# Four message-passing layers on one core: an attention pass with paired short operations, and sage passes of 42 slot groups with one chunk of gathered edges each

## The chip, the cores and the metric

The kernel runs on one core of a Trainium2 chip. The metric is the time of one execution on the device in microseconds (us). Engines are named as in the profile: PE is TensorE's matmuls, PEld its weight loads, DVE VectorE, ACT ScalarE, POOL GpSimd, SP SyncE.

## The reference

12500 nodes with 64 features and 200000 edges, sorted by target. Four layers, each a layernorm, a relu, a graph operation and a residual sum. The change touches the second and third:

```python
# layer 1 (attention), for every edge (row, col), Wh = h @ W + b
sim = dot(Wh[row], Wh[col]) / max(|Wh[row]| * |Wh[col]|, 1e-8)
weight = adj * softplus(...) * (row != col) * (c0 * relu(sim) - c1 * relu(-sim))
prop = segment_sum(weight[:, None] * Wh[col], row)
# layer 2 (sage, applied twice)
mean = segment_sum(h[src], dst) / max(deg, 1)
h = relu(mean @ W_l + b_l + h @ W_r)
```

Layer 0 is an edge network (message pass), layer 3 a softmax attention over incoming edges.

## The kernel before

**Two ways to sum over edges.** The message pass and the softmax pass go by *chunks*: 196 chunks of 1024 edges (8 of 128) in the order of the targets. GpSimd gathers the source rows from memory (indirect DMA, 128 rows at a time, 8 for a chunk), a one-hot matrix tells TensorE which of 128 targets from `base_i[c]` on an edge belongs to, and the product is added to `acc`.

The attention pass and the two sage passes go by *slots*, without gathers. The edges are cut into 53 groups of 3840 (`NGR`; the last one adds only 320 edges). Within a group each edge has a slot in one of 49 source blocks of 256 nodes (`NSB`), 128 slots a block. `build_slots` writes, once, a row of slot sources (`srow`, `pair_rows`) and a column of slot targets (`dcol`).

**Sage pass** (`slot_sums`, called twice). The node table `T` lies in SBUF as three bf16 pieces whose sum is the value. `run_steps` writes the program of each engine: in step k each stage with lag l handles item k - l. A group has 25 steps of two source blocks. DVE makes the source one-hots `ohT` for 10 blocks at once (L1685, two operations) and the target one-hots `ohd` for each block (L1691, 256 wide, two per step). PE multiplies `ohT` with `T` (L1728), ACT copies the product from PSUM to `G` (L1717), PE multiplies `ohd` with `G` and sums over the whole group (L1740). Then DVE adds the three pieces (L1701), PE turns the result (L1752) and DVE adds it to a window of 256 columns of `acc` (L1711). Rings of 5 steps tie the engines together: DVE's `ohd` of step k waits for PE's sum of step k - 5.

**Attention pass** (`att_slots`). 49 blocks of source nodes, 8 steps a block; a step takes 7 groups (the last 4) of one block, 392 steps in all. In each, DVE makes four one-hot comparisons (L1524), PE gathers both ends of the edges (L1573) and turns one-hots (L1583, L1590), ACT copies, DVE multiplies (L1532), takes a maximum (L1534) and a sum over 64 features (L1535). From these the weight is made by five short operations on 128 x 7 numbers: reciprocal L1537, product L1540, the two halves L1542 and L1543, their sum L1547. Each waits for the one before. L1503 multiplies rows by the weight, ACT and DVE split the result into three pieces (L1491, L1509, L1496, L1514), and PE sums (L1602).

**Around them.** `phase` runs the node phases (layernorm, weights), 10 groups of nodes each; a phase may also store rows to memory (L349), and waits at its end until they have landed (L623). After the second sage pass a block loads the edge columns of the softmax pass again: targets from the kept copy, sources from the input (L2060 to L2062). Blocks end with all engines meeting.

The round counts (`rounds2_i`) are 1 for the inputs at hand; a pass is repeated only where a block has more than 128 edges of a group or a window is too narrow.

## Time and profile before

| | us |
|---|---|
| median of 3 runs | 9413.38 (9408.04 to 9417.32) |
| the profiled execution | 9405.75 |
| its span, first to last instruction | 9403.0 |
| attention pass, 2805.8 to 4933.1 | 2127.3 |
| first sage pass, 5088.9 to 5976.7 | 887.8 |
| second sage pass, 6142.1 to 7028.1 | 886.0 |
| busy over the span: PE / DVE / ACT / POOL | 7528.1 / 6605.3 / 3741.7 / 3350.5 |

Busy in tenths, in 40 slices of 235 us:

```profile
PE   6577577777768888888886999899995778878777
DVE  3999344444338999999996999689983555555554
ACT  1000222222225656665654777467761222222221
POOL 2677777777500000000000000000001777777774
```

A digit is the busy share of a slice. The attention pass is slices 12 to 20, the sage passes are 21 to 25 and 26 to 29; POOL is idle in all of them. Left of them lies the message pass, right the softmax pass.

### The profile page before, as it was taken

The page shows a single profiled execution, that of the slowest core. Times are in us where ns is not written, and L with a number is a line of the kernel's source. Part 1 is how long each engine was busy: PE and PEld are TensorE (multiplying, and loading weights), DVE is VectorE, ACT ScalarE, POOL GpSimd, SP SyncE. Part 2 cuts the span into 40 slices and gives each one's busy share as a digit, 9 for nine tenths or more (in the row PEclk, how much of TensorE's full clock was granted, in tenths as well). Part 3 has the DMA queues.
Part 4 walks back from the last instruction along what each step waited for, and adds up shares of the span by engine and source line. Part 5 has one row for each costly group of instructions (what it writes and reads, how often), then busy time and mean ns, then how long its engine had stood idle before and what let it go on. Part 6 is the DMA issues. An engine that isn't in the chain of part 4 may idle for free. (4 is left out here: it accounts for less than half of the span.)

```text
span 9403.0 us, 265151 instructions
## 1 busy us (share of the span) xinstructions
PE 7528.1 (80%) x91323; PEld 7064.7 (75%) x91323; DVE 6605.3 (70%) x19944; ACT 3741.7 (40%) x6989; POOL 3350.5 (36%) x3255
## 2 busy tenths in 40 slices
PE   6577577777768888888886999899995778878777
PEld 6344577777657888888876999799984777777776
DVE  3999344444338999999996999689983555555554
ACT  1000222222225656665654777467761222222221
POOL 2677777777500000000000000000001777777774
PEclk9767788888759999999996999799995777777776
DMA  5311222222113222222221333123322111111111
GB/s 64 52 39 40 67 72 73 72 72 73 49 39 101 83 85 84 85 84 84 84 71 48 98 98 98 40 92 99 98 86 24 27 26 26 26 26 26 26 26 29
DMA packets 635318, 586.40 MB, mean 62 GB/s; under 512 B 377638, under 2 KB 481158, under 8 KB 634696
## 3 DMA queue, kind: packets, MB, share of 16 engines
q1 hardware_dynamic: 528824, 461.21, 17.9%
q0 software_dynamic: 104272, 117.41, 6.2%
q8 instruction: 424, 6.95, 0.3%
q10 hardware_dynamic: 1728, 0.25, 0.0%
q14 instruction: 70, 0.57, 0.0%
HBM read 538.95 MB, written 39.60 MB: 62 GB/s over the span
## 5 line engine op out<-in xcount | busy, mean ns | idle before, releaser
L787 POOL DMA_INDIRECT soft_G<-soft,soft_idx x1568 | 1555.6, 992 | 539.1 <-issue 473.0
L657 POOL MEMSET acc<- 96x1280 f32 x30 | 34.4, 1162 | 4638.2 <-POOLq L1330 2447.9
L1717 ACT ACTIVATE sage_G<-ps 128x384 bf16<-128x384 f32 (+1 forms) x2650 | 1284.2, 485 | 508.2 <-PE ps L1728 500.3
L1728 PE MATMUL ps<-T,sage_ohT 128*128 128x192 bf16 x10388 | 1305.5, 247 | 21.4 <-DVE sage_ohT L1685 17.8
L1740 PE MATMUL ps<-sage_G,sage_ohd 128*128 128x192 bf16 x10388 | 1287.1, 245 | 1.0 <-ACT sage_G L1717 1.0
L787 POOL DMA_INDIRECT msg_G<-msg_src,msg_idx x1176 | 1153.1, 981 | 364.2 <-issue 348.7
L1691 DVE TENSOR_SCALAR sage_ohd<-iota,sage_cols 128x256 bf16<-128x256 bf16 x5194 | 1140.8, 282 | 96.1 <-PE ps L1740 66.8
L1573 PE MATMUL ps<-att_far,att_ohT 128*128 128x65 bf16 x15582 | 945.1, 196 | 319.7 <-DVE att_ohT L1524 269.3
L1573 PEld LDWEIGHTS ps<-att_far,att_ohT 128*128 128x128 bf16 x15582 | 689.5, 100 | 389.3 <-DVE att_ohT L1524 283.1
L1573 PE MATMUL ps<-acc,att_ohT 128*128 128x65 bf16 x15582 | 942.0, 196 | 0.5 <-issue 0.5
L1728 PEld LDWEIGHTS ps<-T,sage_ohT 128*128 128x128 bf16 x10388 | 904.8, 98 | 34.6 <-DVE sage_ohT L1685 18.1
L1740 PEld LDWEIGHTS ps<-sage_G,sage_ohd 128*128 128x128 bf16 x10388 | 899.3, 97 | 1.7 <-ACT sage_G L1717 1.4
L896 PE MATMUL ps<-msg_OH,msg_msg 128*65 128x128 f32 x3136 | 475.4, 316 | 376.9 <-ACT msg_msg L941 376.9
L896 PEld LDWEIGHTS ps<-msg_OH,msg_msg 128*65 128x65 f32 x3136 | 420.8, 162 | 392.8 <-ACT msg_msg L941 392.8
L1573 PEld LDWEIGHTS ps<-acc,att_ohT 128*128 128x128 bf16 x15582 | 689.3, 99 | 1.2 <-issue 0.7
L927 DVE TENSOR_TENSOR msg_msg<-ps,msg_G 128x512 f32<-128x512 f32 x196 | 135.4, 691 | 770.5 <-DMA msg_G<-msg_src,msg_idx 761.0
L998 POOL DMA_INDIRECT acc<-msg_src,srci x392 | 526.3, 1343 | 370.5 <-POOLq L306 161.2
L1820 PE MATMUL ps<-ident,soft_G 128*128 128x128 f32 x1568 | 324.6, 375 | 373.2 <-DMA soft_G<-soft,soft_idx 373.2
L941 ACT ACTIVATE msg_msg<-msg_msg 128x512 f32<-128x512 f32 x196 | 123.5, 630 | 1078.2 <-DVE msg_msg L927 1078.2
L1685 DVE TENSOR_SCALAR sage_ohT<-sage_rows,iota_p 128x1280 bf16<-128x1280 bf16 (+1 forms) x1060 | 529.2, 542 | 32.4 <-PE ps L1728 20.4
L1820 PEld LDWEIGHTS ps<-ident,soft_G 128*128 128x128 f32 x1568 | 256.5, 192 | 390.1 <-DMA soft_G<-soft,soft_idx 390.1
L1602 PE MATMUL ps<-att_Vp,att_ohs 128*128 128x192 bf16 x5194 | 493.9, 246 | 9.9 <-issue 5.2
(443 smaller groups left out, 15924.3 us busy)
## 6 DMA issues: line engine op xcount, KB each, us to landing
sage_rows<-srow SPq DMA_DIRECT2D x424, 320.0 KB, 3.3
acc<-pair_rows SPq DMA_DIRECT2D x196, 448.0 KB, 3.7
att_rows<-pair_rows SPq DMA_DIRECT2D x147, 448.0 KB, 3.7
msg_edge<-edge_attr SPq DMA_DIRECT2D x196, 256.0 KB
sage_rows<-srow SPq DMA_DIRECT2D x106, 288.0 KB, 3.3
soft_G<-soft,soft_idx POOLq DMA_INDIRECT x1568
msg_G<-msg_src,msg_idx POOLq DMA_INDIRECT x1176
kept_rows<-acc POOLq DMA_DIRECT2D x49, 256.0 KB, 2.4
```

The lines of the kernel that those rows point to most:

```text
L787: eng.indirect_dma_start(B["G"][h][:, j, :], None, src_table, bass.IndirectOffsetOnAxis(ap=B["idx"][h][:, j:j + 1], axis=0)).then_inc(gath ...
L896: ins = pe.matmul(ps[0:m, 6 + h % 2, 0:P], rows(j), B["OH"][h % HOTS][:, j, :], start=(j == 0), stop=(j == TPC - 1))
L927: dve.tensor_tensor(B["msg"][b][:, :, 0:D], ps[:, 4 + b, :].rearrange("p (j d) -> p j d", d=D), B["G"][h][:], ALU.add).then_inc(S["summed" ...
L998: pool.indirect_dma_start(kept_G[q % KRING][:, j, :], None, msg_src, bass.IndirectOffsetOnAxis(ap=srci[:, kept_chunks[q], j:j + 1], axis=0 ...
L1573: ins = pe.matmul(ps[:, bank + s % 2, c * W65:(c + 1) * W65], ohT[s % 2][:, f, half, c * P:(c + 1) * P], rows_of[:, half, k, :], start=(ha ...
L1602: ins = pe.matmul(ps[:, 4 + s // QS, half * 3 * D:(half + 1) * 3 * D], ohs[s % 4][:, c, half * P:(half + 1) * P], Vp[s % 4][:, c, :], star ...
L1685: ins = dve.tensor_scalar(ohT[b][:, half, 0:w], rows[ring][:, 0:w], iota_p1[:, half:half + 1], None, ALU.is_equal)
L1691: ins = dve.tensor_scalar(ohd[s % RING][:, c, :], iota256[:], cols[s // STEPS][:, 2 * q + c:2 * q + c + 1], None, ALU.is_equal)
L1717: act.activation(G[s % RING][:, 0:m, :], ps[:, s % RING, 0:m * 3 * D].rearrange("p (c n) -> p c n", c=m), ACT.Copy).then_inc(S["taken"], 1)
L1728: ins = pe.matmul(ps[:, s % RING, c * 3 * D:(c + 1) * 3 * D], ohT[b][:, half, at:at + P], T[:, 2 * (2 * q + c) + half, 0:3 * D], start=(ha ...
L1740: ins = pe.matmul(ps[:, 5 + s // STEPS, half * 3 * D:(half + 1) * 3 * D], ohd[s % RING][:, c, half * P:(half + 1) * P], G[s % RING][:, c, ...
L1820: pe.transpose(banks(2)[:, j, :], B["G"][h][:, j, D + 1:D + 2].broadcast_to([P, P]), ident[:])
```

## The change

**Attention.** `t` and `weight` are twice as wide. `dve_weight` is cut in two: `dve_dot` (product, maximum, sum) runs each step and writes its half of `t`; the five short operations run in odd steps only, over both halves. The product by the weight, `dve_v`, moves from lag 1 to lag 2, and ACT's first copy of it, `act_hi`, from the head of its step to the end.

On DVE, attention pass before, from the last operations of one step (`keep` holds the weighted rows, `att_t` the short columns):

```order
L1532 TENSOR_TENSOR acc<-ps,att_C 128x455
L1534 TENSOR_SCALAR att_t<-acc 128x7
L1535 TENSOR_REDUCE att_t<-acc 128x7
L1537 RECIPROCAL att_t<-att_t 128x7
L1540 TENSOR_TENSOR att_t<-att_t 128x7
L1542 SCALAR_TENSOR_TENSOR att_t<-att_t,att_own 128x7
L1543 SCALAR_TENSOR_TENSOR att_t<-att_t,att_own 128x7
L1547 TENSOR_TENSOR att_weight<-att_t 128x7
L1503 TENSOR_TENSOR keep<-att_C,att_weight 128x448
```

The same engine and place now, from the end of one step (up to L1519) over the next one into its chain:

```order
L1555 TENSOR_SCALAR att_t<-acc 128x7
L1556 TENSOR_REDUCE att_t<-acc 128x7
L1519 TENSOR_TENSOR keep<-att_C,att_weight 128x448
L1540 TENSOR_SCALAR att_ohT<-acc,iota_p 128x896 x4
L1525 TENSOR_TENSOR keep<-keep,att_Vp 128x448
L1530 TENSOR_TENSOR att_Vp<-keep,att_Vp 128x7x64
L1552 TENSOR_TENSOR acc<-ps,att_C 128x455
L1555 TENSOR_SCALAR att_t<-acc 128x7
L1556 TENSOR_REDUCE att_t<-acc 128x7
L1565 RECIPROCAL att_t<-att_t 128x14
L1568 TENSOR_TENSOR att_t<-att_t 128x14
L1570 SCALAR_TENSOR_TENSOR att_t<-att_t,att_own 128x14
```

L1519 follows L1556 at once where a step has no chain; the five operations stand in every second step, over 14 columns.

**Sage.** `XG` = 42: only the first 42 groups (161280 edges) go by slots. The last 42 chunks hold the other edges; the first 3 of them and half of the fourth overlap the slot groups, and their targets are set to a number that matches nothing. Each slot group carries one chunk, 42 in a pass. GpSimd issues 8 gathers of 128 rows x 384 bytes for it from a new table `sage_rows` in memory, into one of two buffers. DVE makes a one-hot of the chunk (two operations), PE multiplies 24 times (8 parts, three pieces) into bank 7, and DVE adds the result to `acc`. No group stands behind the loop any more: 21 iterations of two groups.

On DVE in the sage loop now, where a chunk's one-hot is made and a group is added:

```order
L1762 TENSOR_SCALAR sage_chunk_off<-chunk_dst,base_bc 128x8
L1766 TENSOR_TENSOR sage_chunk_oh<-chunk_iota,sage_chunk_off 128x1024
L1109 REGISTER_ALU
L1727 TENSOR_SCALAR sage_ohd<-iota,sage_cols 128x256 x2
L1721 TENSOR_SCALAR sage_ohT<-sage_rows,iota_p 128x1152 x2
L1109 REGISTER_ALU
L1727 TENSOR_SCALAR sage_ohd<-iota,sage_cols 128x256 x2
```

The first two rows are new, once a group; a third new one, `acc<-acc,ps 64x128` (L1777), stands 15 steps behind them. On PE, the products of a chunk stand three at a time behind the two sums of a step:

```order
L1821 MATMUL ps<-sage_G,sage_ohd 128x192 x4
L1789 MATMUL ps<-sage_chunk_oh,sage_chunk_rows 64x128 x3
L1809 MATMUL ps<-T,sage_ohT 128x192 x4
L1821 MATMUL ps<-sage_G,sage_ohd 128x192 x4
L1789 MATMUL ps<-sage_chunk_oh,sage_chunk_rows 64x128 x3
```

This is so in 8 of a group's 25 steps; the first of them waits for the gathers and the one-hot.

**Around.** The two node phases ahead of the sage passes store `T` into `sage_rows`. A block ahead of them loads the chunk columns and builds a comparison table. The source indices are kept in memory in SBUF's layout (`src_kept`) and loaded from there later on. A block ahead of each sage pass sets the chunk bases; GpSimd's semaphores are brought back after it. `slot_rounds` works out a second pair of round counts.

The diff, cut to its core:

```diff
+XG = 42
...
-            sp.dma_start(node_rows(table, g), group_of(T, g) if buf == "T" else src_of[buf][s][:, :, 0:cols]).then_inc(out_sem[k][s], 16)
+            sp.dma_start(node_rows(table, g), group_of(T, g)[:, :, 0:cols] if buf == "T" else src_of[buf][s][:, :, 0:cols]).then_inc(out_sem[k][s], 16)
...
+            dve.tensor_tensor(gstate[:, 12:13], gstate[:, 1:2], small[:, 7:8], ALU.max)
...
-        t, weight, red = buf("t", [P, 6, PC], F32, 1)[0], buf("weight", [P, PC], F32, 4), buf("red", [P, 2, D], F32, 1)[0]
+        t, weight, red = buf("t", [P, 6, 2 * PC], F32, 1)[0], buf("weight", [P, 2 * PC], F32, 2), buf("red", [P, 2, D], F32, 1)[0]
...
-            dve.wait_ge(S["weight"], n + 1)
+            dve.wait_ge(S["weight"], pair_of(i, s) + 1)
             need(dve, S["lo"], n - 3)
-            w = weight[s % 4][:, 0:m].rearrange("p (c o) -> p c o", o=1).broadcast_to([P, m, D])
+            w = weight[s // 2 % 2][:, s % 2 * PC:s % 2 * PC + m].rearrange("p (c o) -> p c o", o=1).broadcast_to([P, m, D])
             dve.tensor_tensor(V[s % 4][:, 0:m, :], C_[s % 4][:, 0:m, 0:D], w, ALU.mult).then_inc(S["v"], 1)
...
+        def dve_dot(dve, i, s):
+            b, q, n, m = place(i, s)
+            at = slice(s % 2 * PC, s % 2 * PC + m)
+            dve.wait_ge(S["taken"], n + 1)
+            need(dve, S["guard"], n)
+            need(dve, S["dot"], n)
+            dve.tensor_tensor(prod[:, 0:m, :], ps[:, s % 2, 0:m * W65].rearrange("p (c d) -> p c d", d=W65), C_[s % 4][:, 0:m, :], ALU.mult).then_inc(S["prod"], 1)
+            dve.wait_ge(S["prod"], n + 1)
+            need(dve, S["weight"], pair_of(i, s))
+            dve.tensor_scalar(t[:, 0, at].rearrange("p (c o) -> p c o", o=1), prod[:, 0:m, D:W65], 1.0e-8, None, ALU.max).then_inc(S["guard"], 1)
+            dve.tensor_reduce(t[:, 1, at], prod[:, 0:m, 0:D], AX, ALU.add).then_inc(S["dot"], 1)
+
         def dve_weight(dve, i, s):
             b, q, n, m = place(i, s)
-            k = s // QS
-            mine = own[k][:, :, q * PC:q * PC + m]
-            dve.wait_ge(S["taken"], n + 1)
-            dve.tensor_tensor(prod[:, 0:m, :], ps[:, s % 2, 0:m * W65].rearrange("p (c d) -> p c d", d=W65), C_[s % 4][:, 0:m, :], ALU.mult).then_inc(S["prod"], 1)
-            dve.wait_ge(S["prod"], n + 1)
-            dve.tensor_scalar(t[:, 0, 0:m].rearrange("p (c o) -> p c o", o=1), prod[:, 0:m, D:W65], 1.0e-8, None, ALU.max).then_inc(S["guard"], 1)
-            dve.tensor_reduce(t[:, 1, 0:m], prod[:, 0:m, 0:D], AX, ALU.add).then_inc(S["dot"], 1)
+            if s % 2 == 0:
+                return
+            p, w = pair_of(i, s), PC + m
+            mine = own[s // QS][:, :, (q - 1) * PC:(q - 1) * PC + w]
             dve.wait_ge(S["guard"], n + 1)
-            dve.reciprocal(t[:, 2, 0:m], t[:, 0, 0:m]).then_inc(S["recip"], 1)
+            dve.reciprocal(t[:, 2, 0:w], t[:, 0, 0:w]).then_inc(S["recip"], 1)
             dve.wait_ge(S["dot"], n + 1)
-            dve.wait_ge(S["recip"], n + 1)
-            dve.tensor_tensor(t[:, 3, 0:m], t[:, 1, 0:m], t[:, 2, 0:m], ALU.mult).then_inc(S["sim"], 1)
-            dve.wait_ge(S["sim"], n + 1)
-            dve.scalar_tensor_tensor(t[:, 4, 0:m], t[:, 3, 0:m], 0.0, mine[:, 0, :], ALU.max, ALU.mult).then_inc(S["pos"], 1)
-            dve.scalar_tensor_tensor(t[:, 5, 0:m], t[:, 3, 0:m], 0.0, mine[:, 1, :], ALU.min, ALU.mult).then_inc(S["neg"], 1)
-            dve.wait_ge(S["pos"], n + 1)
-            dve.wait_ge(S["neg"], n + 1)
+            dve.wait_ge(S["recip"], p + 1)
+            dve.tensor_tensor(t[:, 3, 0:w], t[:, 1, 0:w], t[:, 2, 0:w], ALU.mult).then_inc(S["sim"], 1)
+            dve.wait_ge(S["sim"], p + 1)
+            dve.scalar_tensor_tensor(t[:, 4, 0:w], t[:, 3, 0:w], 0.0, mine[:, 0, :], ALU.max, ALU.mult).then_inc(S["pos"], 1)
+            dve.scalar_tensor_tensor(t[:, 5, 0:w], t[:, 3, 0:w], 0.0, mine[:, 1, :], ALU.min, ALU.mult).then_inc(S["neg"], 1)
+            dve.wait_ge(S["pos"], p + 1)
+            dve.wait_ge(S["neg"], p + 1)
             need(dve, S["v"], n - 3)
-            dve.tensor_tensor(weight[s % 4][:, 0:m], t[:, 4, 0:m], t[:, 5, 0:m], ALU.add).then_inc(S["weight"], 1)
+            dve.tensor_tensor(weight[s // 2 % 2][:, 0:w], t[:, 4, 0:w], t[:, 5, 0:w], ALU.add).then_inc(S["weight"], 1)
...
-                flow(dve, (0, dve_turned), (3, dve_rest), (4, dve_lo), (6, dve_add), (1, dve_weight), (1, dve_v))
+                flow(dve, (0, dve_turned), (3, dve_rest), (4, dve_lo), (6, dve_add), (1, dve_dot), (1, dve_weight), (2, dve_v))
...
-                flow(act, (2, act_hi), (1, act_one_hots), (3, act_mid), (0, act_take), (0, act_next))
+                flow(act, (1, act_one_hots), (3, act_mid), (0, act_take), (0, act_next), (2, act_hi))
...
-    run_steps(eng, 2 * STEPS, NGR // 2, STEPS, stages)
+    run_steps(eng, 2 * STEPS, XG // 2, 0, stages)
...
+            dve.wait_ge(S["cadd"], g + 1)
             w = acc[0:D, bass.ds(first, SB)]
             dve.tensor_tensor(w, w, ps[0:D, 7, 0:SB], ALU.add).then_inc(S["added"], 1)
+
+        def pool_chunks(pool):
+            for n in range(XG):
+                need(pool, S["csum"], n - 1)
+                for j in range(TPC):
+                    pool.indirect_dma_start(chunk_rows[n % 2][:, j, :], None, sage_rows, bass.IndirectOffsetOnAxis(
+                        ap=chunk_src[:, n, j:j + 1], axis=0)).then_inc(chunk_in[n % 2], 16)
+
+        def dve_chunk(dve, i, s):
+            n, k = i * 2 + s // STEPS, s // STEPS
+            if s % STEPS:
+                return
+            need(dve, S["coh"], n - 1)
+            dve.tensor_scalar(chunk_off[k][:], chunk_dst[:, bass.ds(n, 1), :].rearrange("p o j -> p (o j)"), base_bc[:, bass.ds(n + (C - XG), 1)], None, ALU.subtract).then_inc(S["coff"], 1)
+            need(dve, S["csum"], n - 1)
+            dve.wait_ge(S["coff"], n + 1)
+            pairs = chunk_off[k][:].rearrange("p (a o t) -> p a o t", o=1, t=2).broadcast_to([P, TPC // 2, P, 2])
+            dve.tensor_tensor(chunk_oh[k][:], chunk_iota[:], pairs, ALU.is_equal).then_inc(S["coh"], 1)
+
+        def dve_chunk_add(dve, i, s):
+            n = i * 2 + s // STEPS
+            if s % STEPS:
+                return
+            first = dve.value_load(base_i[0:1, bass.ds(n + (C - XG), 1)], min_val=0, max_val=N)
+            dve.wait_ge(S["csum"], n + 1)
+            need(dve, S["added"], n)
+            need(dve, S["cadd"], n)
+            w = acc[0:D, bass.ds(first, P)]
+            dve.tensor_tensor(w, w, ps[0:D, 7, SB:SB + P], ALU.add).then_inc(S["cadd"], 1)
+
+        def pe_chunk(pe, i, s):
+            n, k, j = i * 2 + s // STEPS, s // STEPS, s % STEPS
+            if j >= TPC:
+                return
+            if j == 0:
+                need(pe, S["added"], n)
+                need(pe, S["cadd"], n)
+                pe.wait_ge(S["coh"], n + 1)
+                pe.wait_ge(chunk_in[k], (i + 1) * (16 * TPC))
+            for part in range(3):
+                ins = pe.matmul(ps[0:D, 7, SB:SB + P], chunk_rows[k][:, j, part * D:(part + 1) * D], chunk_oh[k][:, j // 2, :, j % 2],
+                                start=(j == 0 and part == 0), stop=(j == TPC - 1 and part == 2))
+            if j == TPC - 1:
+                ins.then_inc(S["csum"], 1)
...
-                flow(dve, (0, dve_one_hots), (11, dve_reduce), (21, dve_add))
+                flow(dve, (0, dve_one_hots), (18, dve_chunk), (11, dve_reduce), (21, dve_add), (33, dve_chunk_add))
...
-                flow(pe, (0, pe_gather), (2, pe_sum), (16, pe_turn))
+                flow(pe, (0, pe_gather), (2, pe_sum), (16, pe_turn), (23, pe_chunk))
...
+              [(sage_rows, "T", 3 * D, "pieces", 2)])
...
-sp.dma_start(srci[:, 0:C - 1, :], by_edge(a["src"], 0, C - 1)).then_inc(again, 16)
-sp.dma_start(srci[:, C - 1:C, :], by_edge(a["src"], E - CE, 1)).then_inc(again, 16)
-sp.wait_ge(again, 48)
+sp.dma_start(srci[:].rearrange("p c j -> p (c j)"), src_kept[:]).then_inc(again, 16)
```

## Rows read from the trace of the kernel before

**Rows 1.** Busy by stretch: us, PE, PEld, DVE, ACT, POOL, clock, DMA share, GB/s.

```profile
2805.80:4933.10 2127.30, 1819.09 (x41552) 1744.30 (x41552) 1957.61 (x5978) 1258.46 (x2056) 0.00 (x0) 0.97 0.27 85
5088.90:5976.70 887.80, 881.51 (x10494) 874.30 (x10494) 825.66 (x3233) 642.12 (x1325) 0.00 (x0) 1.00 0.32 97
5200.00:5900.00 700.00, 697.23 (x8326) 692.09 (x8324) 654.29 (x2565) 509.41 (x1051) 0.00 (x0) 1.00 0.33 98
6142.10:7028.10 886.00, 882.29 (x10494) 875.07 (x10494) 825.67 (x3233) 642.12 (x1325) 0.00 (x0) 1.00 0.32 97
```

**Rows 2.** Waits from 5200 to 5900 us: total, times, longest.

```profile
DVE sage_ohd L1691 <- PE ps L1740: 24.4, 84, 0.4
DVE sage_ohT L1685 <- PE ps L1728: 10.1, 21, 0.5
```

**Rows 3.** Groups by shape, same stretch: busy us, mean ns, idle before, releaser.

```profile
L1691 DVE TENSOR_SCALAR sage_ohd<-iota,sage_cols 128x256 bf16<-128x256 bf16 x2059 | 452.0, 282 | 35.6 <-PE ps L1740 24.4
L1685 DVE TENSOR_SCALAR sage_ohT<-sage_rows,iota_p 128x1280 bf16<-128x1280 bf16 x338 | 171.1, 550 | 10.1 <-PE ps L1728 10.1
L1701 DVE TENSOR_REDUCE sage_red<-ps 128x128 f32<-128x384 f32 x42 | 23.2, 552 | 0.0
```

**Rows 4.** Timeline of the attention pass at 3504 us: start, length, instruction.

```profile
3503.94 0.19 DVE L1537 RECIPROCAL att_t<-att_t 128x7 f32<-128x7 f32 x1
3504.41 0.46 PEld L1583 LDWEIGHTS ps<-ident_b,att_ohT 128*128 128x128 bf16 x8
3504.83 0.38 PEld L1590 LDWEIGHTS ps<-ident_b,att_ohT 128*128 128x128 bf16 x6
3504.97 0.63 DVE L1503 TENSOR_TENSOR keep<-att_C,att_weight 128x448 f32<-128x448 f32 x1
```

**Rows 5.** Wait of TensorE in the attention pass, 2900 to 4800 us.

```profile
PE ps L1573 <- DVE att_ohT L1524: 252.2, 267, 2.3
```

**Rows 6.** The reciprocal of the attention pass at two widths.

```profile
L1537 DVE RECIPROCAL att_t<-att_t 128x7 f32<-128x7 f32 x311 | 60.1, 193 | 0.0
L1537 DVE RECIPROCAL att_t<-att_t 128x4 f32<-128x4 f32 x45 | 7.6, 168 | 0.0
```

**Rows 7.** GpSimd's gathers: of 300 to 900 us, and of 7300 to 9300 us.

```profile
L998 POOL DMA_INDIRECT acc<-msg_src,srci x297 | 418.4, 1409 | 162.9 <-DMA kept_rows<-acc 83.8 <-issue 79.1
...
L787 POOL DMA_INDIRECT soft_G<-soft,soft_idx x1542 | 1530.6, 993 | 469.9 <-issue 465.7 <-DVE soft_msg L1888 2.7 <-ACT soft_idx L874 1.5
```

**Rows 8.** One line each, all its instructions: min/median/max ns.

```profile
L1860 DVE TENSOR_SCALAR soft_q<-soft_q,soft_win x196: 218/220/461, 7286.6 to 9308.6; 128x2 f32<-128x2 f32 x196
...
L413 DVE TENSOR_SCALAR enter_st<-enter_st x10: 172/172/16002, 25.7 to 178.1; 128x10 f32<-128x10 f32 x10
```

**Rows 9.** Operations like those added: two by line, one from the costliest groups.

```profile
L1208 DVE TENSOR_TENSOR slots_fields<-slots_oh,acc x159: 903/905/921, 286.6 to 936.5; 128x1470 bf16<-128x1470 bf16 x159
...
L1224 DVE TENSOR_TENSOR slots_ohslot<-count_slot,slots_slot x53: 2157/2158/2193, 293.1 to 941.4; 128x3840 bf16<-128x3840 bf16 x53
...
L905 DVE TENSOR_TENSOR acc<-acc,ps 65x128 f32 x196 | 55.6, 284 | 52.2 <-issue 42.4 <-PE ps L896 8.9
```

**Rows 10.** Timeline at two ends of node phases, the first with a store.

```profile
2788.52 0.84 DVE L443 TENSOR_TENSOR T<-after_msg_rN,T 128x650 bf16<-128x650 f32 x1 [0.82 <-ACT T L507]
2799.11 0.36 SPq L1609 DMA_DIRECT2D keep<-bcol  x1
...
5082.48 0.82 DVE L443 TENSOR_TENSOR T<-after_att_xc,T 128x640 bf16<-128x640 f32 x1
5085.04 0.35 SPq L1671 DMA_DIRECT2D sage_cols<-dcol  x1
```

**Rows 11.** Timeline after the second sage pass, and one transfer's issue to landing.

```profile
7064.63 0.33 SPq L2060 DMA_DIRECT2D dstf_again<-dst_kept  x1
7084.10 1.27 ACT L489 ACTIVATE after_sage_accS<-acc 65x1280 f32<-65x1280 f32 x1 [25.35 <-PEq L2057]
...
dstf_again<-dst_kept SPq DMA_DIRECT2D x1, 784.0 KB, 4.5
```

More of the change, by code:

```diff
@@ L81, in gnn_kernel @@
         dst_kept = dram("dst_kept", (P, C * TPC))
+        src_kept = dram("src_kept", (P, C * TPC), I32)
+        sage_rows = dram("sage_rows", (NPAD, 3 * D), BF16)
         rec_b = dram("rec_b", (NGR, P, KF * TG), BF16)
@@ L112, in gnn_kernel @@
         rounds2_i = sb("rounds2_i", [1, 1], I32)
+        rounds3_i = sb("rounds3_i", [1, 1], I32)
+        rebuild3_i = sb("rebuild3_i", [1, 1], I32)
         rebuild_i = sb("rebuild_i", [1, 1], I32)
@@ L1354, in slot_rounds, with next_slots @@
             dve.drain()
-        def next_slots(dve):
+            dve.tensor_tensor(gstate[:, 12:13], gstate[:, 1:2], small[:, 7:8], ALU.max)
+            dve.drain()
+            dve.tensor_tensor(gstate[:, 13:14], gstate[:, 4:5], gstate[:, 12:13], ALU.mult)
+            dve.drain()
+            dve.tensor_scalar(gstate[:, 14:15], gstate[:, 13:14], 1.5, float(NGR - 1), ALU.is_gt, ALU.mult)
+            dve.drain()
+            dve.tensor_scalar(gstate[:, 14:15], gstate[:, 14:15], 1.0, None, ALU.add)
+            dve.tensor_copy(rounds3_i[:], gstate[0:1, 13:14])
+            dve.drain()
+            dve.tensor_copy(rebuild3_i[:], gstate[0:1, 14:15])
+            dve.drain()
+        def next_slots(dve, windows=1):
             r, wrap, w, last = (gstate[:, k:k + 1] for k in (7, 8, 9, 10))
@@ L1366, in next_slots @@
             dve.drain()
-            dve.tensor_tensor(last, w, gstate[:, 1:2], ALU.is_lt)
+            dve.tensor_tensor(last, w, gstate[:, windows:windows + 1], ALU.is_lt)
             dve.drain()
@@ L1451, in act_block @@
                             need(act, S["gathered"], b * QS - QS)
-                            need(act, S["weight"], b * QS - QS)
+                            need(act, S["weight"], b * (QS // 2) - QS // 2)
                             hold(act)
@@ L1651, in place, with _ @@
                     return g, q, i * (2 * STEPS) + s, min(2, NSB - 2 * q)
+                with nc.Block() as block:
+                    @block.vector
+                    def _(dve):
+                        move_bases(dve, True)
                 with nc.Fori(0, rounds) as r:
@@ L1749, in pe_turn @@
                             need(pe, S["added"], g)
+                            pe.wait_ge(S["cadd"], g + 1)
                             hold(pe)
@@ L1769, in _ @@
                                 flow(act, (0, act_take))
+                            @block.gpsimd
+                            def _(pool):
+                                pool_chunks(pool)
                             @block.tensor
                             def _(pe):
-                                flow(pe, (0, pe_gather), (2, pe_sum), (16, pe_turn))
+                                flow(pe, (0, pe_gather), (2, pe_sum), (16, pe_turn), (23, pe_chunk))
                         with nc.Block() as block:
+                            @block.gpsimd
+                            def _(pool):
+                                for q in chunk_in:
+                                    pool.wait_ge(q, XG // 2 * (16 * TPC))
+                                pool.inc_swdge_sem(chunk_in, [XG // 2 * (16 * TPC)] * 2, mode="sub")
                             @block.sync
@@ L2043, in gnn_kernel, with _ @@
         att_slots()
+        chunks_kept = ExitStack()
+        chunk_src = chunks_kept.enter_context(nc.sbuf_tensor("chunk_src", [P, XG, TPC], I32))
+        chunk_dst = chunks_kept.enter_context(nc.sbuf_tensor("chunk_dst", [P, XG, TPC], F32))
+        chunk_iota = chunks_kept.enter_context(nc.sbuf_tensor("chunk_iota", [P, TPC // 2, P, 2], BF16))
+        first_edge = XG * GE - (C - XG) * CE
+        whole, part = first_edge // CE, first_edge % CE // TPC
+        assert XG % 2 == 0 and 0 <= first_edge and whole < XG and part % 32 == 0
+        s_chunks, s_masked = sem("chunk_columns"), sem("chunks_masked")
+        with nc.Block() as block:
+            @block.sync
+            def _(sp):
+                sp.dma_start(chunk_src[:].rearrange("p c j -> p (c j)"), src_kept[:, (C - XG) * TPC:]).then_inc(s_chunks, 16)
+                sp.dma_start(chunk_dst[:].rearrange("p c j -> p (c j)"), dst_kept[:, (C - XG) * TPC:]).then_inc(s_chunks, 16)
+                sp.wait_ge(s_chunks, 32)
+            @block.vector
+            def _(dve):
+                dve.tensor_copy(chunk_iota[:], iota_f[:].rearrange("p (o n t) -> p o n t", o=1, t=1).broadcast_to([P, TPC // 2, P, 2])).then_inc(s_masked, 1)
+                dve.wait_ge(s_chunks, 32)
+                if whole:
+                    dve.memset(chunk_dst[:, 0:whole, :], -4.0 * P).then_inc(s_masked, 1)
+                if part:
+                    dve.memset(chunk_dst[0:part, whole, :], -4.0 * P).then_inc(s_masked, 1)
         phase("after_att", "prop", {"v": [(1, "xc"), (1, "var"), (2, "rest"), (2, "own"), (1, "h"), (2, "lo")],
@@ L2050, in gnn_kernel @@
                                        "p": [(1, "mean"), (2, "own"), (1, "turned")]},
-              [])
+              [(sage_rows, "T", 3 * D, "pieces", 2)])
         slot_sums("sage2")
+        chunks_kept.close()
         tables.close()
```

20 lines of the change are left out of this document (14 added, 6 removed).

## The prediction

> **What bounds the kernel now.** I began with the busy digits in 40 slices and cut the span into stretches. The change works in three of them: the attention pass (2127.3 us) and the two sage passes (887.8 and 886.0 us) [rows 1]. The message pass before them and the softmax pass behind them, both paced by GpSimd's gathers, keep their code.
>
> In the middle of a sage pass TensorE is busy for 697.23 of 700.00 us [rows 1]; 42 groups end in that stretch (one reduction each [rows 3]), so a group lasts 16.67 us and TensorE works 16.60 of them. VectorE is close behind: it waits for TensorE 24.4 + 10.1 us there [rows 2], 0.82 us a group, so its own work is 15.85 us. The reader is to see two engines that lie 5% apart: whatever shortens one hands the pass to the other.
>
> In the attention pass it is the other way round: TensorE is busy 1819.1 of 2127.3 us [rows 1] and waits for VectorE's one-hots [rows 5], while VectorE shows hardly a wait for another engine. Its 392 steps (49 blocks of 8) take 5.4 us each. VectorE sets that time.
>
> **Attention: one chain of short operations for two steps.** From the start of the reciprocal to the start of the product that uses the weight VectorE needs 3504.97 - 3503.94 = 1.03 us [rows 4]: five operations on 7 columns, each waiting for the one before. Two steps now share one chain over 14 columns. Width costs little: the reciprocal goes from 168 to 193 ns for 3 more columns [rows 6], so 7 more are 0.06 us, and I give the other four 0.04 together. A pair saves 2 x 1.03 - 1.13 = 0.93 us, 196 pairs save 182 us. What hides the rest: TensorE's 1819 us fit into the 1945 that remain. The product comes one step later and ScalarE copies it at the end of its step instead of the beginning; VectorE's subtraction, which needs that copy, has the four comparisons of the next step ahead of it. If that cover is thin in some steps, a few us go. Bounds 0 and 182; I take 178.
>
> **Sage: 42 groups instead of 53.** 11 groups go from each pass: at the old pace 11 x 16.67 = 183 us a pass. Each remaining group carries one chunk of 1024 edges.
>
> TensorE gets 24 products of 128 columns. Eight weight loads of such products take 3504.83 - 3504.41 = 0.42 us start to start [rows 4], 0.0525 each, so 1.26 us: 16.60 + 1.26 = 17.86 us a group.
>
> VectorE gets an offset (0.22 us, as L1860 [rows 8]), a comparison over 1024 elements (905 ns at 1470 and 2158 at 3840 elements give 0.53 ns an element, so 0.67 us [rows 9]) and an addition from PSUM (0.28 us, L905 [rows 9]): 1.17 us, hence 15.85 + 1.17 = 17.02 us.
>
> GpSimd gets 8 gathers a group: 993 ns each plus 466/1542 = 0.30 us between two, so 10.4 us; beside the slot building, where VectorE is all but full, 1409 ns and 13.4 us [rows 7]. Both fit into 17.9.
>
> By these sums TensorE would still set the pace. What they leave out is that the two engines disturb each other. A VectorE operation that takes 218 ns at least takes up to 461 when gathers run [rows 8]: a gather holds it up by as much as 0.24 us. In that pass VectorE is mostly doing something else; in the sage pass 93% of its time is busy (654.29 of 700 [rows 1]), nearly all in tensor_scalar operations like that one [rows 3], so that nearly every gather will hit one. The cost for 8 gathers lies between 0 and 1.9 us a group from these rows; I take 0.2 us each, near the top, 1.6 us. VectorE then needs 18.6 us and takes the pace from TensorE by 0.7. A pass: 53 x 16.67 = 883.5 becomes 42 x 18.6 = 781.2, 102.3 less, both 204.6.
>
> The Trainium skill, SBUF — State Buffer, "SBUF: two separate sides", says more than these rows: a VectorE instruction in a 2-port mode and a GpSimd instruction exclude each other for their whole length. The trace agrees for computing instructions (a tensor_scalar of 172 ns took 16002 at the start [rows 8], where GpSimd fills count tables) but not for gathers: 461 ns at most, against gathers of 993. What the whole rule would do is the slower rival below.
>
> **What stands around the passes.** Two node phases now write their table to memory. A phase that does so ends 2799.11 - 2789.36 = 9.75 us behind its last table entry, one that does not 5085.04 - 5083.30 = 1.74 us [rows 10]: +8.0 each, 16. The block that moves the bases ahead of each pass: a change of block is that 1.74, with its operations 3 us, twice 6; 0 and 10 are the bounds. The block that loads the chunk columns: less than half of a 784 KB load, which lands in 4.5 us [rows 11], with its block 6 (3 to 8). Keeping the source indices: another store beside the first, 3 (0 to 4.5). Six more short operations on the round counts: 1.5. Longer tails of both passes, with the semaphore subtraction: 4 (1 to 10). Against it, the sources come back from the kept copy: the old load held everything up for 7084.10 - 7064.63 = 19.5 us; two plain loads should take 7.5, so -12. Together +24.5 us, between 10 and 40.
>
> **Sum.** It is made against the profiled execution, 9405.75 us (span 9403.0): 9405.75 - 178 - 204.6 + 24.5 = 9047.7. The median of the runs is 7.6 us above that execution, so 9055 us as a median.
>
> **Rivals.**
> - TensorE keeps the pace (0.18). Waits for the port fall into the 0.82 us that VectorE has spare, a group takes 17.9: 2 x (883.5 - 751.8) = 263 instead of 205, 8997 us. For it: most gathers in the last pass leave short operations at their median of 220. Against it: VectorE is never that free here.
> - GpSimd starves (0.18). VectorE's operations follow each other without a gap and a gather waits until that row breaks; TensorE then waits for the chunk's rows, and only in that wait does VectorE leave gaps. The mean of 1409 ns beside a full VectorE [rows 7] speaks for some of it. With groups between 18.6 and 22.9, say 20.8 us, both passes gain 2 x (883.5 - 873.6) = 20: 9240 us.
> - The attention gain fails (0.06), because ScalarE's later copy holds up VectorE by as much as was saved: 9055 + 178 = 9233 us. For it: ScalarE is 59% busy with long copies [rows 1]; against it: it has 2 us a step to spare.
> - Slower than before (0.08). A gather keeps VectorE out for its whole 0.99 us. Nearly all of VectorE's operations there are of the kind that can be kept out, so 8 x 0.99 = 7.9 us a group, 17.02 + 7.9 = 24.9 us: 2 x (883.5 - 1045.8) = -325, and 9055 + 205 + 325 = 9585 us. It decides from 22.9 us a group, where the two passes' 1767 us and the other parts' gain of 153.5 are used up ((1767 + 153.5) / 84), that is from 0.73 us lost per gather. This is what the skill's rule of exclusion gives with durations from rows; the 461 ns speak against it. The same page has a gather-side price, 620 ns alone against some 3100 beside a VectorE copy; by that an estimate of 8 x 3.1 = 24.8 us a group on GpSimd would also be slower.
>
> **How the numbers follow.** The forecast has 0.50, and its own range is 9015 to 9110. TensorE's case adds the low side, starvation and the failed attention gain the high side up to some 9235; beyond lie half of starvation and the slower case, and a little below 8975. So 8975 to 9235. About 0.2% (19 us) is what a measurement of this kernel can tell from none. Faster by more: all cases but the last, less a little of starvation's far end, 0.91; same 0.02; slower 0.07.
>
> **What would show it.** In the changed profile: the five short operations with 196 instances each and an attention pass near 1950 us; sage groups counted by their reduction (42 in a pass), 18.6 us apart, with TensorE at some 96% busy instead of 99.6 and waiting for VectorE's one-hots; VectorE's 256-wide comparisons with a mean above 282 ns; gathers between 1.0 and 1.6 us; the chunk's product never waiting for its gathers; 8 us between the last table entry and the pass. The forecast is wrong if TensorE stays at 99% (too high), if TensorE waits for gathers or the comparisons' mean passes some 340 ns (too low), or if VectorE waits for ScalarE in the attention pass.

## The result, and the profile after

The changed kernel takes 9139.98 us (median of 4 runs, 9133.8 to 9148.12), the kernel before 9414.31 (4 runs beside it). The ratio is 0.971, 95% interval 0.9693 to 0.9727. The forecast was 9055, with a range of 8975 to 9235. The profiled execution took 9133.8 us, its span 9132.0.

Busy time by stretch of the changed kernel (us, then PE, PEld, DVE, ACT, POOL, granted clock, DMA share, GB/s), to be held against [rows 1]: the attention pass, the first sage pass, its middle, the second sage pass.

```profile
2817.90:4765.30 1947.40, 1791.03 (x41552) 1726.21 (x41552) 1819.28 (x4999) 1259.69 (x2055) 0.00 (x0) 0.98 0.31 93
4928.80:5765.30 836.50, 832.84 (x9324) 739.94 (x9324) 704.03 (x2689) 508.99 (x1050) 525.46 (x334) 1.00 0.37 101
5200.00:5700.00 500.00, 499.73 (x5606) 443.77 (x5604) 422.98 (x1617) 306.21 (x633) 326.13 (x203) 1.00 0.37 102
5931.10:6767.80 836.70, 833.28 (x9324) 740.16 (x9324) 703.70 (x2689) 508.99 (x1050) 516.57 (x333) 1.00 0.37 101
```

Three things stand there. The attention pass fell by 179.9 us, from 2127.3 to 1947.4. The sage passes fell by only 51.3 and 49.3. And in their middle TensorE is busy for 499.73 of 500 us while VectorE fell to 85%: TensorE sets the pace, more than before. Spans differ by 271.0 us; with 280.5 from the passes, what stands around them costs 9.5.

Waits of the changed kernel in the middle of the sage pass (total us, times, longest), against [rows 2]:

```profile
ACT sage_G L1798 <- PE ps L1809: 192.2, 628, 0.8
POOL sage_chunk_rows L1754 <- PE ps L1789: 119.5, 25, 6.4
DVE sage_ohd L1727 <- PE ps L1821: 58.6, 124, 0.6
PEld ps L1789 <- issue: 31.6, 201, 0.2
PEld ps L1809 <- DVE sage_ohT L1721: 3.6, 15, 0.3
```

All others wait for TensorE, GpSimd too: it waits for the chunk products of two chunks ago, and TensorE never for a gather. One row is new in kind: the weight loads of the chunk products (L1789) stand behind a gap of 0.16 us on average (31.6 us in all), 201 times, that is once for each triple (eight a group). They are not loaded ahead.

Groups by shape in the same stretch (busy us, mean ns, idle before), against [rows 3]:

```profile
L1754 POOL DMA_INDIRECT sage_chunk_rows<-sage_rows,chunk_src x203 | 327.6, 1614 | 174.0 <-PE ps L1789 119.5 <-issue 54.6
L1727 DVE TENSOR_SCALAR sage_ohd<-iota,sage_cols 128x256 bf16<-128x256 bf16 x1236 | 274.9, 284 | 58.9 <-PE ps L1821 58.6
L1789 PE MATMUL ps<-sage_chunk_oh,sage_chunk_rows 128*64 128x128 bf16 x601 | 72.0, 227 | 0.0
L1737 DVE TENSOR_REDUCE sage_red<-ps 128x128 f32<-128x384 f32 x25 | 13.5, 541 | 0.0
```

25 reductions in 500 us give only a rough pace. Finer are the 256-wide comparisons, 49 a group (2059 of them are the 42 groups of [rows 3]): 1236 are 25.2 groups, so a group takes 19.8 us, where I had 18.6 and for TensorE alone 17.86. VectorE's comparison went from 282 to 284 ns. Where TensorE's time goes, two stretches of its own timeline show (start, length, instruction): a step without chunk products, and one with three.

```profile
5301.34 0.49 PE L1821 MATMUL ps<-sage_G,sage_ohd 128*128 128x192 bf16 x4
5301.67 0.33 PE L1809 MATMUL ps<-T,sage_ohT 128*128 128x192 bf16 x2
...
5303.34 0.49 PE L1821 MATMUL ps<-sage_G,sage_ohd 128*128 128x192 bf16 x4
5303.76 0.36 PE L1789 MATMUL ps<-sage_chunk_oh,sage_chunk_rows 128*64 128x128 bf16 x3
5304.05 0.34 PE L1809 MATMUL ps<-T,sage_ohT 128*128 128x192 bf16 x2
```

From the four L1821 to the next L1809 it is 0.33 us, with three products between them 0.71: three products cost 0.38 us, not 3 x 0.0525 = 0.16. Eight times a group that is 3.04 us instead of 1.26. The shape column has the clue: 128*64, the weights are 64 columns wide, among products whose weights are 128 wide.

The short operations of the attention pass, against [rows 6], and the wait that was to be feared there (2900 to 4700 us):

```profile
L1565 DVE RECIPROCAL att_t<-att_t 128x14 f32<-128x14 f32 x139 | 32.0, 230 | 0.0
L1575 DVE TENSOR_TENSOR att_weight<-att_t 128x14 f32<-128x14 f32 x139 | 24.2, 174 | 14.9 <-DVE att_t L1571 4.4
```

```profile
PE ps L1601 <- DVE att_ohT L1540: 98.7, 186, 1.2
DVE keep L1525 <- ACT att_Vp L1507: 15.8, 29, 1.6
```

TensorE's wait for one-hots fell from 252.2 [rows 5] to 98.7 us. VectorE does wait for ScalarE now, 29 times, for 15.8 us in all.

### The profile page after: what moved, and what is told of

The parts are those of the page before. It is cut to its first block and busy times, and to the rows that moved or that the text cites. A ratio compares the mean times of both kernels' runs of the same rounds, so it can differ in the third digit from the quotient of the medians.

```text
span 9132.0 us, 256071 instructions
## 1 busy us (share of the span) xinstructions
PE 7411.1 (81%) x88983; PEld 6783.6 (74%) x88983; DVE 6231.9 (68%) x17891; ACT 3478.7 (38%) x6439; POOL 4407.7 (48%) x3927
## 5 line engine op out<-in xcount | busy, mean ns | idle before, releaser
L1754 POOL DMA_INDIRECT sage_chunk_rows<-sage_rows,chunk_src x672 | 1047.7, 1559 | 732.4 <-PE ps L1789 410.2
L662 POOL MEMSET acc<- 96x1280 f32 x30 | 34.4, 1162 | 2573.7 <-POOLq L2147 2270.4
L1798 ACT ACTIVATE sage_G<-ps 128x384 bf16<-128x384 f32 (+1 forms) x2100 | 1018.0, 485 | 677.4 <-PE ps L1809 671.2
L1809 PE MATMUL ps<-T,sage_ohT 128*128 128x192 bf16 x8232 | 1041.6, 248 | 26.8 <-DVE sage_ohT L1721 25.8
L1727 DVE TENSOR_SCALAR sage_ohd<-iota,sage_cols 128x256 bf16<-128x256 bf16 x4116 | 917.3, 284 | 196.8 <-PE ps L1821 195.2
L1821 PE MATMUL ps<-sage_G,sage_ohd 128*128 128x192 bf16 x8232 | 1020.1, 245 | 0.0
L1809 PEld LDWEIGHTS ps<-T,sage_ohT 128*128 128x128 bf16 x8232 | 668.7, 98 | 107.3 <-DVE sage_ohT L1721 38.5
L1821 PEld LDWEIGHTS ps<-sage_G,sage_ohd 128*128 128x128 bf16 x8232 | 712.2, 97 | 0.6
```

The source lines that it names most:

```text
L1727: ins = dve.tensor_scalar(ohd[s % RING][:, c, :], iota256[:], cols[s // STEPS][:, 2 * q + c:2 * q + c + 1], None, ALU.is_equal)
L1754: pool.indirect_dma_start(chunk_rows[n % 2][:, j, :], None, sage_rows, bass.IndirectOffsetOnAxis(ap=chunk_src[:, n, j:j + 1], axis=0)).the ...
L1798: act.activation(G[s % RING][:, 0:m, :], ps[:, s % RING, 0:m * 3 * D].rearrange("p (c n) -> p c n", c=m), ACT.Copy).then_inc(S["taken"], 1)
L1809: ins = pe.matmul(ps[:, s % RING, c * 3 * D:(c + 1) * 3 * D], ohT[b][:, half, at:at + P], T[:, 2 * (2 * q + c) + half, 0:3 * D], start=(ha ...
L1821: ins = pe.matmul(ps[:, 5 + s // STEPS, half * 3 * D:(half + 1) * 3 * D], ohd[s % RING][:, c, half * P:(half + 1) * P], G[s % RING][:, c, ...
```

## The experiments

Eleven times a kernel was timed, on four chips; each is compared with the kernel before on the same chip. On chip 7 the kernel before takes 9415 us, as it did in the result above: I call this the first kind. On chips 8, 6 and 12 it takes 10289, 10343 and 10286 us: the second kind. That difference became a finding of its own.

| kernel | kind (chip) | us | ratio to before (95%) |
|---|---|---|---|
| attention alone | second (8) | 10103.3 | 0.982 (0.980 to 0.983) |
| wide weights | second (8) | 10280.3 | 0.998 (0.997 to 1.000) |
| adjacent elements | second (8) | 10553.6 | 1.025 (1.023 to 1.027) |
| one step | second (8) | 10632.2 | 1.033 (1.032 to 1.035) |
| changed kernel | first (7) | 9133.3 | 0.970 (0.968 to 0.971) |
| one step | first (7) | 9028.0 | 0.959 (0.958 to 0.961) |
| swapped roles | first (7) | 8938.1 | 0.950 (0.949 to 0.951) |
| two chunks gathered | first (7) | 9132.3 | 0.969 (0.968 to 0.971) |
| swapped, two gathered | second (6) | 9880.5 | 0.955 (0.953 to 0.956) |
| swapped roles | second (6) | 10675.8 | 1.032 (1.030 to 1.034) |
| changed kernel | second (12) | 10560.9 | 1.026 (1.024 to 1.028) |

**Attention alone.** The kernel before with the diff's hunks in `att_slots` only.

> The attention change alone; the sage passes, the stores and all else are as before. The trace gives the attention pass 1947.3 us instead of 2127.3. Theory (the pass gains by itself, and the sage part is what fell short): 9414 - 180 = 9234 us, and the sage passes last 888 and 886 us. Rival (part of the 180 us is due to what else was changed, or is given back after the pass): above 9250 us.

10289.3 to 10103.3: 186 us, where 180 was expected, though the base was another. The attention pass took 1945.6 us (3317.0 to 5262.6) and the sage passes 886.7 and 885.1. So this part gains by itself, and by about the same amount on a slower chip.

**Wide weights.**

```diff
-ins = pe.matmul(ps[0:D, 7, SB:SB + P], chunk_rows[k][:, j, part * D:(part + 1) * D], chunk_oh[k]...
+ins = pe.matmul(ps[:, 7, SB:SB + P], chunk_rows[k][:, j, part // 2 * D:part // 2 * D + 2 * D], chunk_oh[k]...
```

> The changed kernel with weights of 128 columns instead of 64 in the chunk's 24 products (each takes two neighbouring pieces, so the product has 128 rows instead of 64); same number of products, same one-hots, same gathers. Its sums are not the reference's, since pieces are taken twice. Theory A (narrow weights are the cost: they are not loaded ahead, and going from 128 to 64 columns and back costs 172 ns a triple): a product falls from 0.14 to about 0.055 us, TensorE needs 17.9 us a group instead of 20.0, and the time is 9140 - 84 x 2.1 = 8964 us; if VectorE beside the gathers needs 18.6 us, as I had forecast, 9022 us. Theory B (the one-hot is read with a step of two elements, and that makes a product dear): no change, 9140 us.

The time, expected at 8964 or 9022 us on a chip of the first kind, was never taken there. On this chip it settles nothing: the engines are held up in the sage passes (below), and the order of the times does not follow TensorE's work (wide weights 10280, adjacent elements 10554, one step 10632 us). TensorE's timeline in a stretch at full clock (1.00 from 5640 to 5680 us) does settle it:

```profile
5663.52 0.49 PE L1821 MATMUL ps<-sage_G,sage_ohd 128*128 128x192 bf16 x4
5663.85 0.34 PE L1789 MATMUL ps<-sage_chunk_oh,sage_chunk_rows 128*128 128x128 bf16 x3
5664.02 0.33 PE L1809 MATMUL ps<-T,sage_ohT 128*128 128x192 bf16 x2
```

0.50 us instead of 0.71: three wide products cost 0.17 us, 0.057 each. That is my price of 0.0525, nearly. Theory A holds for this stretch; its effect on the time follows from the runs on chip 7.

**Adjacent elements.**

```diff
-chunk_oh[k][:, j // 2, :, j % 2]
+chunk_oh[k][:, j // 2, j % 2 * D:(j % 2 + 1) * D, :].rearrange("p n t -> p (n t)")
```

> The changed kernel, but each chunk product reads 128 neighbouring elements of the one-hot instead of every second one of 256. Its sums are not the reference's, since the elements are in another order. Theory B (the step is the cost): 8964 to 9022 us. Theory A (narrow weights): 9140 us, no change. A mixture, with the step making 18 of the 70.6 ns between two products of a triple: 24 x 0.018 = 0.43 us a group, 9104 us.

```profile
5800.90 0.49 PE L1821 MATMUL ps<-sage_G,sage_ohd 128*128 128x192 bf16 x4
5801.32 0.35 PE L1789 MATMUL ps<-sage_chunk_oh,sage_chunk_rows 128*64 128x128 bf16 x3
5801.61 0.34 PE L1809 MATMUL ps<-T,sage_ohT 128*128 128x192 bf16 x2
```

0.71 us, as with every second element. Reading every second element costs nothing that this shows; theory B falls. The 9140 us expected by theory A could not be seen on this chip (10554).

**One step.** The 24 products of a chunk one behind the other.

```diff
-if j >= TPC: return
+if j: return
 ...
-for part in range(3):
+for j in range(TPC):
+    for part in range(3):
```

> The changed kernel with the 24 chunk products of a group in one step, one behind the other, instead of three in each of eight steps: one change from 128 to 64 columns and back a group instead of eight. Theory A1 (the change between the two widths costs 172 ns each time): 7 x 0.172 = 1.2 us a group less, 9140 - 101 = 9039 us. Theory A2 (a narrow product costs 0.14 us wherever it stands) and theory B (the step): 9140 us.

Its timeline, on chip 8 (10632 us, where 9039 or 9140 stood for a chip of the first kind):

```profile
5927.00 0.49 PE L1821 MATMUL ps<-sage_G,sage_ohd 128*128 128x192 bf16 x4
5927.42 1.55 PE L1790 MATMUL ps<-sage_chunk_oh,sage_chunk_rows 128*64 128x128 bf16 x24
5928.90 0.34 PE L1809 MATMUL ps<-T,sage_ohT 128*128 128x192 bf16 x2
```

24 products cost 1.90 - 0.33 = 1.57 us, three cost 0.38. With a price p for a product and e for going to narrow weights and back, 24p + e = 1.57 and 3p + e = 0.38: p = 0.057, e = 0.21 us. A narrow product costs what a wide one does; the eight changes of width a group cost 8 x 0.21 = 1.7 us. Two equations for two unknowns prove nothing yet. The test is what they say of the time on a chip of the first kind, together with the control:

> The changed kernel once more, beside the other kernels of this call, because the chip of the first four runs took 10289 us for the kernel before instead of 9414. On a chip like the first: ratio 0.971 to the kernel before. On one like the second: the first four runs had ratios of 0.982 (attention alone), 1.025 (adjacent elements, whose triples last as long as those of the changed kernel) and 1.033 (one step), so the changed kernel should be near 1.025 there, slower than before. If the ratio is 0.971 there too, the edits and not the chip explain those two.

> The 24 chunk products in one step again. In its first trace the 24 products follow each other at 57.9 ns, with 176 ns ahead of the first and 151 behind the last, against three at 70.5 ns with the same two edges, eight times, in the changed kernel. TensorE saves 7 x (0.176 + 0.151 - 0.082 - 0.058) = 1.3 us a group by that, so 18.6 us instead of 20.0. On a chip like the first: 9140 - 84 x 1.35 = 9027 us, if no other engine takes over (VectorE at 18.6, as I had forecast, would give the same). On a chip like the second: near 1.033 of the kernel before.

Control: 9133.3, ratio 0.970, as expected. One step: 9028.0 where 9027 was expected; only the order of TensorE's program differs. The sage passes took 785.1 and 786.3 us instead of 836. VectorE at my 18.6 us a group would have given the same time, so it needs one run more to tell these two apart.

**Swapped roles.** The one-hot is the weight, the rows are streamed. VectorE reduces the three pieces (a second small operation beside L1737), TensorE turns the result.

```diff
-for part in range(3):
-    ins = pe.matmul(ps[0:D, 7, SB:SB + P], chunk_rows[k][:, j, part * D:(part + 1) * D], chunk_oh[k][:, j // 2, :, j % 2], ...)
+ins = pe.matmul(ps[:, 7, SB:SB + 3 * D], chunk_oh[k][:, j // 2, :, j % 2], chunk_rows[k][:, j, :], start=(j == 0), stop=(j == TPC - 1))
...
+dve.tensor_reduce(chunk_red[k][:], ps[:, 7, SB:SB + 3 * D].rearrange("p (k d) -> p d k", d=D), AX, ALU.add)
+pe.transpose(ps[0:D, 7, SB:SB + P], chunk_red[k][:], ident[:])
```

> The chunk's one-hot becomes the weights (128 columns) and the gathered rows (192 columns) are what is streamed: 8 products of the usual shape a group instead of 24 narrow ones, then a reduction by VectorE, a turn by TensorE, and the addition as before. TensorE: 16.60 + 8 x 0.084 + 0.3 (turn, with its edges) = 17.6 us; VectorE 16.9 + 0.35 = 17.3. If the edges of narrow weights are the whole excess: 17.7 us a group and 9140 - 84 x 2.3 = 8947 us on a chip like the first. If VectorE beside gathers needs 18.6 + 0.35 us, as my forecast had it: 9052 us. If the chain reduction, turn, addition holds up the group's own turn (all use one bank): 9140 or more.

8938.1 us, where 8947 was expected: 5.0% under the kernel before and the fastest of all. The middle of its first sage pass, 5000 to 5600 us: busy time, and the counts of one operation a group.

```profile
5000.00:5600.00 600.00, 599.15 (x7129) 590.95 (x7126) 578.22 (x2238) 416.47 (x862) 366.98 (x277) 1.00 0.42 116
```

```profile
L1728 DVE TENSOR_SCALAR sage_ohd<-iota,sage_cols 128x256 bf16<-128x256 bf16 x1685 | 373.5, 288 | 3.7
L1738 DVE TENSOR_REDUCE sage_red<-ps 128x128 f32<-128x384 f32 x34 | 18.7, 549 | 0.0
L1775 DVE TENSOR_REDUCE sage_chunk_red<-ps 128x64 f32<-128x192 f32 x34 | 12.2, 358 | 11.8 <-PE ps L1805 11.8
```

1685 comparisons are 34.4 groups in 600 us, 17.4 us each. VectorE does all its work, one reduction more, beside all eight gathers, and is busy for 578.22 / 34.4 = 16.8 us of them. My forecast of 18.6 us for it (19.0 with that reduction) is refuted here, in a pass where it is 96% busy: the whole group is shorter.

**Two chunks gathered.**

```diff
-for n in range(XG):
+for n in range(2):
 ...
-pe.wait_ge(chunk_in[k], (i + 1) * (16 * TPC))
+pe.wait_ge(chunk_in[k], 16 * TPC)
```

> The changed kernel with the gathers of the first two chunks only in each pass; the later products use those rows again, so its sums are not the reference's. If TensorE alone sets the pace and gathers cost the others nothing: no change on a chip like the first, 9140 us. If gathers take time from VectorE that shows in the end: up to 42 x 2 x 0.3 = 25 us less. On a chip like the second, where the gathers seem to hold up everything: the sage passes fall to 836 us each as on the first chip, and the ratio to the kernel before to (10289 - 180 - 100 + 10) / 10289 = 0.974.

9132.3 against 9133.3 us: on chip 7 640 of 672 gathers cost the time nothing that can be measured. The middle of the sage pass without them (5200 to 5700 us), and VectorE's comparison, which takes 284 ns with them:

```profile
5200.00:5700.00 500.00, 499.95 (x5612) 444.16 (x5611) 419.14 (x1614) 305.82 (x632) 0.00 (x0) 1.00 0.26 82
L1727 DVE TENSOR_SCALAR sage_ohd<-iota,sage_cols 128x256 bf16<-128x256 bf16 x1235 | 273.2, 275 | 62.0 <-PE ps L1821 61.8
```

9 ns on 49 comparisons is 0.44 us a group, 0.055 us a gather. That is an upper bound, since VectorE's operations overlap: seven comparisons of 284 ns stand in 1.47 us of the changed kernel's timeline at 5301.58. By busy time the gathers cost it 422.98 - 419.14 = 3.8 us in 25 groups with 203 gathers, 0.02 us each. I had taken 0.2.

**The second kind of chip.** Three runs go with the question why the same kernel loses there.

> The kernel with swapped roles (one-hot as weights), with the gathers of the first two chunks only in each pass; later products use those rows again, so its sums are not the reference's. It was 8938 us with all gathers on a chip like the first, where TensorE was busy 599.15 of 600 us and VectorE 578.22. If gathers take next to nothing from VectorE and TensorE: 8938 us, within 15. If they take 0.2 us each, as I had forecast, VectorE falls to 15.7 us a group and the time stays, since TensorE holds 17.6. On a chip like the second, if gathers in flight hold up the other engines: it keeps the whole gain, ratio near 0.955 to the kernel before, where the version with gathers does not.

> The kernel with swapped roles and all gathers once more, beside the one without. On a chip like the first: ratio 0.950 to the kernel before, again. On one like the second: a group needs about as long as in the other kernels with gathers there; with 1.025 and 1.033 for kernels whose TensorE work is 20.0 and 18.6 us a group, the pace there is not TensorE's work, and I expect 1.00 to 1.03.

> The changed kernel itself, to have its ratio on a chip of the second kind. If the kernel before takes some 10300 us: gathers hold up the other engines there, the kernel with adjacent elements (same pace by TensorE) had 1.025 and the one with swapped roles 1.032 with gathers and 0.955 without, so the changed kernel should have 1.025, that is slower than before. If gathers were not the cause, and it was something in those edits, it should have 0.97. On a chip of the first kind (9414 us for the kernel before): 0.970 once more.

The changed kernel is slower than before there, 1.026 (chip 12). On chip 6 the swapped one gains 4.5% without most of its gathers (sage passes 748.5 us each) and loses 3.2% with them (1148 and 1146 us). Besides the gathers these two differ only in that TensorE no longer waits for later gathers, and no such wait of TensorE shows in the trace with them. VectorE without them is busy for 384.59 us in 400, or 23.1 groups: 16.6 us a group beside 16.8 with them on chip 7, where 0.2 us a gather would have given 15.7. Waits of the changed kernel on chip 12, 5700 to 6100 us of its first sage pass:

```profile
ACT sage_G L1798 <- PE ps L1809: 203.9, 321, 2.4
DVE sage_ohd L1727 <- PE ps L1821: 109.5, 129, 3.8
PE ps L1821 <- issue: 41.8, 28, 3.4
ACT sage_G L1798 <- remote: 16.8, 7, 3.8
```

Single waits are up to 3.8 us long between PE, ACT and DVE, which had the longest at 0.8 in the result's trace. One of them in the timeline, within a run of eight gathers (issued from 5715.98 to 5729.51):

```profile
5725.34 0.51 PE L1809 MATMUL ps<-T,sage_ohT 128*128 128x192 bf16 x4
...
5726.02 0.50 PE L1809 MATMUL ps<-T,sage_ohT 128*128 128x192 bf16 x4
...
5727.01 0.95 POOL L1754 DMA_INDIRECT sage_chunk_rows<-sage_rows,chunk_src  x1 [0.30 <-issue]
...
5727.80 0.49 ACT L1798 ACTIVATE sage_G<-ps 128x384 bf16<-128x384 f32 x1 [2.26 <-PE ps L1809]
5728.26 0.94 POOL L1754 DMA_INDIRECT sage_chunk_rows<-sage_rows,chunk_src  x1 [0.30 <-issue]
```

ScalarE copies the result of the product that began at 5725.34 and ended at 5725.85, and starts 1.95 us after that end; in the result's trace such a copy starts 0.04 us after it (a product from 5300.16 for 0.50 us, its copy at 5300.70). TensorE then has nothing to sum, and the granted clock is 0.90 over these 400 us:

```profile
5700.00:6100.00 400.00, 337.40 (x3396) 286.18 (x3395) 262.71 (x982) 179.45 (x383) 148.70 (x120) 0.90 0.27 78
```

The swapped kernel without most of the gathers, same stretch, on chip 6 (with them the clock is 0.81 there and TensorE busy for 296.88 us):

```profile
5700.00:6100.00 400.00, 400.00 (x4778) 396.05 (x4777) 384.59 (x1502) 279.09 (x578) 0.00 (x0) 1.00 0.30 94
```

That the gathers cost the time there is shown by the pair on chip 6. What in them does it (the signals from their descriptors, their traffic, or GpSimd's own work on them) is open: no run separates these.

## Why the prediction came out as it did

The time lay in the range, 85 us above the forecast, and outside the forecast's own 9015 to 9110. That it lay in the wide range is in part luck: the side above 9110 stood for starving gathers and a failed attention gain, and neither happened. By its steps, in the profiled execution:

- *Attention, -178.* Measured -179.9, and alone 186. One chain for two steps, 196 of them. The reciprocal went from 193 to 230 ns, 0.037 us where I had 0.06; the wait for ScalarE, for which I allowed 4 us, is 15.8 us in 1800, as the cover is thin in some steps, and other savings that I did not trace make up for it. Right in mechanism and in the sum.
- *TensorE, 17.86 us a group.* **This is the step that failed.** I took the 24 products at 0.0525 us each from eight weight loads that follow one another in the attention pass [rows 4]. For wide weights that price holds (0.057). But these are 64 wide and stand three by three among products with 128, and each such triple costs 0.21 us more: 3.04 us a group instead of 1.26. With 16.60 that makes 19.6 of the 19.8; the last 0.2 I did not trace. The shape of the products stood in the change, and [rows 4] has only full-width ones; I read a duration and not the shape beside it.
- *VectorE, 18.6 us a group and setting the pace.* Wrong. It is busy for 422.98 / 25.2 = 16.8 us, where 654.29 / 42 = 15.6 and the three new operations (1.17) make 16.75 without a charge for the gathers. (My 17.02 also counted small gaps; by that count it is 17.5, and 0.55 of this is a gap before the new addition, L1777, 13.9 us in 25 times, that I had left out.) The 461 ns of [rows 8] were the worst of many, and I charged nearly that excess to each gather: 0.2 us, where at most 0.055 was measured. The two errors partly hid each other: the 1.6 us charged to VectorE stood where 1.8 us were missing on TensorE. With both engines priced right TensorE alone gives 19.6.
- *The passes, -204.6.* Measured -100.6. That is 104 us too little: 84 groups x 1.2 us are 101; each pass after is 5 us longer than 42 x 19.8 = 831.6, for its start and end; against it, the passes before were 887.8 and 886.0 us long, where 53 x 16.67 gave 883.5. The 15 us of the next point and 2 of attention took some of it back, and 86 us of error were left in the profiled execution.
- *Around them, +24.5.* Measured +9.5. Ahead of the attention pass +12.1 (10.5 forecast: chunk columns, kept sources, short operations). From the last table entry to the pass 10.9 us in place of 6.5, and about the same the second time: +4.4 and +4.1, where 11 stood each time; other parts of these gaps moved by -4 to +3 us, which I did not follow up. The store costs less than the one of [rows 10] suggested. The reload, timeline of the changed kernel:

```profile
6809.21 0.33 SPq L2180 DMA_DIRECT2D dstf_again<-dst_kept  x1
6809.58 0.49 SPq L2181 DMA_DIRECT2D srci_again<-src_kept  x1
6816.06 2.43 ACT L494 ACTIVATE after_sage_accS<-acc 65x1280 f32<-65x1280 f32 x2 [13.66 <-PEq L2177]
```

6.9 us from first issue to the next phase, where it was 19.5 [rows 11]: -12.6 for my -12.

- *Rivals.* "TensorE keeps the pace" named the right engine and had the wrong price (17.9). GpSimd did not starve: its gathers rose to 1559 ns over all 672, inside the 1.0 to 1.6 I gave (1614 in the middle of the pass), and it waits for TensorE. The slower rival (0.99 us a gather) is refuted on the first kind of chip by the 0.055. On the second kind the outcome had its sign, but not by its mechanism: VectorE's comparison takes 284 ns there too (chip 12, the stretch above), so it isn't kept out, it waits.
- *Signs.* "TensorE at 96% and waiting for one-hots" was the one to watch. I had written that TensorE at 99% would mean my number was too high. It stayed at 99.9%, and the number was too low, because I thought only of a cheaper rival and not of dearer products. The sign "VectorE waits for ScalarE in the attention pass" did come, with 15.8 us, and the pass still gained what was forecast: a wait without a size was no good sign.

The Trainium skill, TensorEngine Tiling (Array Packing), "Key Properties", says that a change of tiling mode drains the engine. The trace agrees if going from 128*128 to 128*64 is such a change, which no run here shows: 0.21 us for going there and back. What happens in the engine in that time is open; shown is only that the cost comes with the change of width.

## What to carry over

Price an added product by its shape and by what stands beside it: one with weights of another width costs its columns plus the edge each time the width changes, so keep equal widths together or swap the operands until the wide one is the weight. Where two engines lie within a few per cent, an error in either price decides, so look for the missing cost on both, the fuller one first. Where a change brings gathers into a stretch that had none, time it on more than one chip before calling it a gain.
